# Summing a block's new rows in their own buffer: the residual add moved from the load buffer into the buffer that the scatters read

## The reference

```
x = layernorm(x + mamba(x))     # in_proj, causal conv of 4 taps, a scan over 2048 steps with 16 states
                                # for each of 512 channels, gate, out_proj
x = layernorm(x + moe(x))       # shared expert + the best 2 of 16 experts, weighted by sigmoid scores
```

## Time and profile before

| | |
|---|---|
| median of 3 runs | 2224.75 us |
| time of the profiled execution | 2220.81 us |
| its span, first to last instruction | 2218.9 us |
| TensorE clock granted, mean | 0.981 of full |
| PE busy | 2062.6 us, 93% |
| DVE busy | 1825.4 us, 82% |
| POOL busy | 1778.1 us, 80% |
| ACT busy | 1741.5 us, 78% |
| last scan's unit ends, second block starts | about 1861 us |

### The profile page before, as it was taken

One profiled execution on the slowest core, in us unless ns is written; L12 is line 12 of the kernel. 1 busy time (PEld: TensorE's weight loads), 2 busy tenths in 40 slices (PEclk: granted clock), 3 DMA queues, 4 the chain that ended last, 5 costly groups with the idle time before them and its releaser, 6 DMA issues. The chain is left out here.

```text
span 2218.9 us, 68067 instructions
## 1 busy us (share of the span) xinstructions
PE 2062.6 (93%) x26118; PEld 1246.7 (56%) x26118; DVE 1825.4 (82%) x3055; ACT 1741.5 (78%) x3561; POOL 1778.1 (80%) x1699
## 2 busy tenths in 40 slices
PE   6899999999999999999999999999999796999996
PEld 2455555555555555555555555555555454788864
DVE  2898899989898989899989898988898994655556
ACT  4888888888888888898989897979898872555537
POOL 2787898979898989898989898988898994566654
PEclk9999999999999999999999999999999999999999
DMA  2232323332333232333232333232323354496668
GB/s 89 68 100 78 109 92 110 92 110 96 111 92 114 88 118 88 110 91 116 88 118 86 113 91 114 90 117 83 114 90 101 103 173 150 139 284 208 194 209 284
DMA packets 152301, 267.42 MB, mean 121 GB/s; under 512 B 26408, under 2 KB 65324, under 8 KB 151470
## 3 DMA queue, kind: packets, MB, share of 16 engines
q1 hardware_dynamic: 137198, 220.93, 33.2%
q0 software_dynamic: 14784, 42.16, 5.4%
HBM read 205.62 MB, written 57.39 MB: 119 GB/s over the span
## 5 line engine op out<-in xcount | busy, mean ns | idle before, releaser
L617 POOL TENSOR_TENSOR hc<-h,c_rep 128x512 f32<-128x512 f32 x1024 | 1286.4, 1278 | 212.5 <-DVE h L1175 164.9
L1175 DVE TENSOR_TENSOR_SCAN h<-g_ps,carry,h 128x512 f32<-128x512 f32 x1024 | 1274.4, 1273 | 71.7 <-ACT h L691 54.1
L691 ACT ACTIVATE h<-dt,a_mat 128x512 f32<-128x512 f32 x1024 | 695.4, 714 | 108.0 <-POOL hc L617 44.6
L969 PEld LDWEIGHTS g_ps<-b_steps,x_conv_rows 64*64 64x64 f32 x16384 | 477.1, 134 | 299.6 <-issue 209.9
L969 PE MATMUL g_ps<-b_steps,x_conv_rows 64*64 64x128 f32 x16384 | 559.0, 274 | 29.8 <-DVE h L1175 24.7
L930 PE MATMUL y_ps<-hc,dg_inv 64*64 64x512 f32 x2048 | 502.8, 605 | 14.8 <-POOL hc L617 6.5
L931 PE MATMUL y_ps<-hc,dg_inv 64*64 64x512 f32 x2048 | 501.4, 605 | 0.0
L930 PEld LDWEIGHTS y_ps<-hc,dg_inv 64*64 64x64 f32 x2048 | 139.5, 135 | 234.1 <-issue 160.4
L1662 POOL DMA_INDIRECT y_planes<-gathered,home x144 | 140.0, 972 | 106.2 <-DVE gathered L2089 81.8
L1855 PE MATMUL banks<-w_up,gathered 128*128 x576 | 148.3, 380 | 2.4 <-ACT gathered L1712 2.4
L1166 DVE TENSOR_TENSOR g_ps<-g_ps,minus_u 128x16 f32<-128x16 f32 x512 | 87.0, 170 | 76.5 <-PE g_ps L969 55.9
(11 more groups left out here) (277 smaller groups left out, 2879.0 us busy)
## 6 DMA issues: line engine op xcount, KB each, us to landing
c_rep<-bc_rows SPq DMA_DIRECT2D x512, 256.0 KB
gathered<-slot_rows SPq DMA_DIRECT2D x144, 129.5 KB, 2.3
gathered<-y_planes SPq DMA_DIRECT2D x32, 512.0 KB, 8.4
w_up<-in_x_t SPq DMA_DIRECT2D x16, 512.0 KB, 4.8
x_raw<-in_x_tok SPq DMA_DIRECT2D x16, 512.0 KB, 4.9
out<-x_t SPq DMA_DIRECT2D x16, 512.0 KB, 3.1
x_t_rows<-y_gated SPq DMA_DIRECT2D x15, 512.0 KB, 4.3
x_t<-x_t_rows POOLq DMA_DIRECT2D x12, 512.0 KB, 5.4
```

The lines of the kernel that those rows point to most:

```text
L617: nc.gpsimd.tensor_tensor(hc[:, at_all % HCS], h[:, at_all % SLOTS], c_rep[:, at % CS], ALU.mult).then_inc(hc_ready, 1)
L691: nc.scalar.activation(h[:, (ITEMS * u + m) % SLOTS], dt[:, c], ACT.Exp, scale=a_mat[:, c, s:s + 1]).then_inc(factor_ready, 1)
L969: one = nc.tensor.matmul(g_ps[some, e, r * T + k * P:r * T + (k + 1) * P], x_rows[rows, c, k, some], steps_of, start=True, stop=True)
L1175: nc.vector.tensor_tensor_scan(slot, du, slot, carry[:, batch(u), c, s:s + 1], ALU.add, ALU.mult).then_inc(scanned, 1)
```

## The change

The sum of out_proj and input rows is written to x_tok instead of back into x_raw, the statistics are taken from x_tok, and the scaling works in place in x_tok. So x_raw is free once the two sums are made, and SP's wait for its reload is for `emptied` of o0 and o1, not for `normed`. In return x_tok is written at m = 20 by DVE and no longer at m = 25 by ACT, so the wait for `scattered` moves from ACT, ahead of L830, to DVE, ahead of o0's sum.

```diff
                     if m == TOKENS_AT and u >= 0:
-                        wait(sp, normed, count(u, TT, 0))
+                        if u > 0:
+                            emptied_all(sp, u, ["o0", "o1"])
                         sp.dma_start(x_raw[:], d["x_tok"][u]).then_inc(x_tok_in, 16)
...
                 act.wait_ge(shifted, count(pu, 2, 2))
-                wait(act, scattered, 16 * 2 * TT * pu)
                 for tt in range(TT):
-                    nc.scalar.activation(x_tok[:, tt], x_raw[:, tt], ACT.Identity, scale=spread[:, tt:tt + 1],
+                    nc.scalar.activation(x_tok[:, tt], x_tok[:, tt], ACT.Identity, scale=spread[:, tt:tt + 1],
                                          bias=kept.shift[:, tt:tt + 1]).then_inc(normed, 1)
...
                 if k == 0:
                     dve.wait_ge(x_tok_in, count(pu, 16, 16))
+                    wait(dve, scattered, 16 * 2 * TT * pu)
                 dve.wait_ge(filled[bank], tiles_before(u, t) + 1)
                 two = slice(2 * k, 2 * k + 2)
-                nc.vector.tensor_tensor(x_raw[:, two], work[:, bank].rearrange("p (a b) -> p a b", a=2), x_raw[:, two],
+                nc.vector.tensor_tensor(x_tok[:, two], work[:, bank].rearrange("p (a b) -> p a b", a=2), x_raw[:, two],
                                         ALU.add).then_inc(emptied[bank], 1)
                 dve.wait_ge(emptied[bank], tiles_before(u, t) + 1)
                 for tt in (2 * k, 2 * k + 1):
-                    nc.vector.bn_stats(stats[:, tt], x_raw[:, tt]).then_inc(norm_step, 1)
+                    nc.vector.bn_stats(stats[:, tt], x_tok[:, tt]).then_inc(norm_step, 1)
```

## The result

The changed kernel takes 2253.96 us in the median of four runs (2242.13 to 2256.95), the kernel before 2223.41 in its four: a ratio of 1.0128, 95% interval 1.01 to 1.0156. It is slower by 1.3%; the medians differ by 30.5 us. The profiled execution was a quick one of its kind, 2241.39 us with a span of 2239.3, so the traces differ by 20.4 us, and the medians by 10 more. Both parts need an explanation.

The account below looks back on a forecast made before the run. Four engines, DVE, POOL, ACT and PE, all nearly full, pass items through short rings. 12 x 1.4 + 2.8 + 5.0 = 24.6 us over the median 2224.75 predict 2249 us; forecast band 2243 to 2257, 8-in-10 range 2238 to 2264.

Parts of the forecast that it names:

- What bounds it, and what is removed: Four nearly full engines bound the kernel; removing ACT's wait and SP's wait for the scaled rows gains 0.
- Changed operands: First sum writing rows of pitch 259, statistics and scaling of unchanged size: at most 0.6 us, taken as 0.
- The stall: DVE's wait for the last scatter before the first sum: 2.8 us in units 3 to 14, 4.2 and 6.4 in 2 and 15.
- What of it is lost: Slacks of 1.0 us at PE's z3 and 0.4 at ACT's copy leave 1.4 us lost in each middle unit, 24.6 in all.
- What DVE does meanwhile: After the second sum DVE is 1.8 us late, its waits of 0.26 and 0.45 absorb the difference, and it ends 1.4 late.
- (a): The slacks of PE and ACT aren't there, the whole stall is lost: 2269 us; 0.2 together with the late landing.
- its late landing: Scatter lands later, stall 3.8 us, losing 36.6 us: 2261 us; 0.2 together with (a).
- (b): DVE's waits for ACT late in the unit give part back, 1.4 shrinking to 0.5 or so: 2236 us; chance 0.1.
- (c): POOL sets the pace and its stored 7.4 us of work hide DVE's pause: not slower, 2225 us; chance 0.05.
- (d): The scatter is done when DVE reaches the first sum, so the change does nothing: 2225 us; chance 0.01.
- (e): An earlier free x_raw or ACT's list without a wait gains something; chance 0.02.

Follow-up runs that it names:

- split_wait: Changed kernel, but the first sum waits only for its own two row groups' scatters, the second for the last two; 0.9982, then 0.9997 times the kernel before.
- two_buffers: Changed kernel with two row buffers for even and odd units and no x_raw, DVE waiting for no scatter; 1.0009 times the kernel before.
- wait_alone: Kernel before plus only DVE's wait for the scatters ahead of the first sum; 1.0144 times the kernel before.
- late_filled: scatter_late with six products that add zeros on PE ahead of z3's wait, from unit 2; 1.0219 times the kernel before.
- after_look: The changed kernel unaltered, profiled once more beside the kernel before; span 2277.3 us against 2236.6.
- scatter_late: Changed kernel with the last scatter at m = 17 in place of 15; 1.0208 times the kernel before.

## Why the prediction was right, and where it was not

The forecast was 2249 us, 24.6 over the median before; measured were 2253.96 and 30.5, inside the range.

By the sum itself a stall of 2.3 to 3.3 us in each unit gives 2242 to 2256 us, not 2243 to 2257.

**What bounds it, and what is removed.** Right. ACT's wait cost nothing, SP's neither: split_wait has both removals and no gain.

**Changed operands: 0.** Right in the sum, by split_wait and two_buffers. L1204's median is 0.69 us in the changed kernel, but it is also 0.69 in wait_alone, which writes x_raw.

**The stall: 2.8 us, 4.2 in unit 2 and 6.4 in unit 15, 44.2 in all.** The place and the number of the waits were right and the size 12% too high: the idle time in the new profile is 39.6, with 2.3 to 2.5 in ten of the twelve middle units, 3.40 and 3.12 in the other two (7 and 13), and 3.90 and 4.96 in units 2 and 15. The 0.5 us from the last packet to the start of the sum was right: in units 3 to 14 of the new trace it is 0.48 to 0.62. What was too long is the time of the packets, taken for all twelve from unit 4 of the trace before.

**What of it is lost: the stall less 1.4.** The rule held. In the ten middle units without a fall of the clock the loss is the stall less 1.38 to 1.47, and in late_filled the stall less 1.1 to 1.5, for stalls of 3.8 to 5.5 us. By it the 39.6 us lose 20.0. That PE sets it is what the rows of unit 4 show: z3 late by 1.56 and z1 by 1.05, and then DVE by 1.05.

**What DVE does meanwhile.** Here a step was wrong, without effect on the sum. I let DVE be 1.8 us late and its waits of 0.26 and 0.45 take up the rest; "no busy time changes". In fact DVE was 1.45 late at the second sum but only 0.3 late at item 22, and the 0.26 grew to 1.00. The add of 128x4 numbers in between took 1.30 us before and takes 0.16 now. In all 15 units together it took 18.5 us and takes 2.4, more than the 12.5 by which DVE's busy time fell. What DVE gains there it loses again in its wait for PE's fill.

**The term that was missing: PE's clock.** I wrote that from about 558 us on all four engines are late by the same 1.4, and did not count the clock at all. But PE stands still in the stall, and the clock is part of the unit's time. Behind three of the four longest stalls it fell at once and cost 1.7 to 2.7 us beyond the rule, 6 us in all; behind the 3.90 of unit 2 it did not. Elsewhere the profiled execution had 41 us at half clock where that of before had 48, and got 5 us back. So its 20.4 us agree with the 20.0 of the rule by luck.

The medians differ by 10 us more than the rule gives, and how much of that is the clock is not settled. Twenty-nine executions of the changed kernel had mean clocks of 0.965 to 0.980, in the middle 0.975, and spans of 2238 to 2267 us; a line through them has 1.75 us for each 0.001. At 0.981, the clock of the one execution of the kernel before that was traced beside them, it gives 2239.5, 20.6 over the span before, and at 0.975 it gives 10 more. That would make it 20 us of stalls and 10 of clock, if the kernel before ran at 0.981 as a rule. But that execution was the quickest of its four. On the two chips of the experiments the clock of 50 executions of the kernel before is known, and in the middle it is 0.976 to 0.977. There it is 0.975 in five executions of the changed kernel and 0.971 in six of wait_alone. At one and the same mean clock, 0.977, the changed kernel took 2269.65 and 2272.84 us and the kernel before, in five executions beside it, 2238.4 to 2246.6: some 26 us apart, where the rule gives 24.0 for the stalls of its trace (43.6 in 14). So on that chip a lower mean clock is a few us of the difference, not 10. Shown is that the wait alone brings all of the 1.4%, that the rule covers 20 to 24 us of it, and that the clock falls behind some stalls.

**The rivals.** (a), the whole stall lost at 2269, falls by the table of units, and its late landing, 3.8 us, by the stalls themselves. (b), part given back later in the unit, falls by the units' lengths, from one unit's first scan to the next one's: without a fall of the clock they are 112.7 to 112.9 us after (units 3, 4, 8 and 14) and 111.5 to 111.9 before, 1.1 more. (c) falls by the same table; POOL's wait, named as what decides, grew, to 1.88 and not to the 3.3 I had written, since the quick 128x4 add let DVE reach item 22 only 0.3 late. (d) falls by the 14 waits. (e): nothing gained, in the two runs of the split wait and in two_buffers. What no rival had is the clock.

Open is why the falls of the clock at the units' ends last 6.8 us more often when a stall lies 60 us back (in 9 of units 1 to 14 in after_look and 8 in wait_alone, though in 3 of the first trace of the changed kernel, against 2 and 5 in the two traces of the kernel before), and why the falls that late_filled avoids return there. The falls themselves are seen, their rule isn't.

## What to carry to other kernels

A wait costs what the engine's queue behind it holds up, less the slack of the engines that wait for it (here 1.4 us, in two steps through PE and ACT), and both can be read from the trace before: look up when the awaited transfer's packets end, not when its instruction does. If a wait has to move forward, split it so that each consumer asks only for the pieces it overwrites; here that took the cost from 1.3% to nothing that the timing can tell. A stall in which TensorE stands still can have a second price, in TensorE's clock, and it need not show right behind the stall; so look at the granted clock, in more than one execution of each kernel, before you divide a difference among causes.

## What the runs showed of the hardware

- TensorE's granted clock was at the lower of its two levels, 1.2 GHz, for 3.4 us right behind two of the changed kernel's stalls and for 6.8 behind a third; PE had stood idle just before for 2.1 us in one piece in unit 7, 1.9 in unit 13 and 3.5 in unit 15. It stayed at 2.4 GHz behind the eleven others: PE's pause was 1.0 to 1.2 us in ten of them, and 2.6 in that of unit 2, whose stall is 3.90. So the length of the pause alone does not decide it. In scatter_late it fell behind each of twelve stalls of 3.8 to 4.1 us, with pauses of PE of 2.6 to 2.9; in late_filled, with PE at work in stalls of 3.8 to 5.5 us, behind none. In scatter_late a fall cost some 1.6 us beyond the stall less 1.4.
- An add of two 128x4 operands in SBUF on DVE took 1.0 to 1.5 us in 14 of 15 units of the kernel before, where POOL was in the midst of a 128x512 product, and 0.16 us in all 15 units of the changed kernel, where in 14 of them the stall had moved it. Each of the 14 slow ones began while a product of POOL was under way and ended 0.02 to 0.03 us behind that product's end; none of the 16 quick ones met a product. The line in both kernels:

```profile
L1214 DVE TENSOR_TENSOR spread<-spread,mean_var x15: 165/1298/1525, 205.5 to 1786.3; 128x4 f32<-128x4 f32 x15
```

```profile
L1215 DVE TENSOR_TENSOR spread<-spread,mean_var x15: 161/163/165, 205.1 to 1806.6; 128x4 f32<-128x4 f32 x15
```

  The first is of the kernel before and the second of the kernel after. The Trainium skill (SBUF — State Buffer, its section Who interferes with whom) says that a DVE op with both inputs in SBUF contends with GpSimd's reads. These rows agree in kind. No run changed POOL's work there by itself, so the cause rests on the two times that fall together.
- A scatter of 128 rows of 1036 bytes, whose issue takes POOL 1.0 us, let the waiting sum start 3.5 to 3.7 us after that issue began in ten units of the changed kernel, where it stands 2.5 us behind another scatter and 155 to 174 packets of the loads ran meanwhile. In units 3 to 14 of scatter_late, where it stands 5 us behind the other one and the loads had 14 to 49 packets, it was 2.6 to 2.8 us. Which of the two makes the difference was not tried. In unit 15, where SP asked for weights 0.3 us after the issue began, it was 5.7 us in the changed kernel and 7.1 to 7.4 in four other executions.
